# Windowed attention and a routed feed-forward: row maxima one unit further ahead, router logits in quarters, fewer signals from TensorE, a rearranged start

## The reference

```python
x = layernorm(x + attention(x))
x = layernorm(x + ffn(x))
# attention: 16 heads of 8 features, windows of 64 tokens with stride 32
# (7 windows and one more at the end, the same tokens as the seventh)
scores = einsum('bhnqd,bhnkd->bhnqk', qw, kw) * scale + pos_bias
ow = einsum('bhnqk,bhnkd->bhnqd', softmax(scores), vw)   # overlapping windows are averaged
attention = merged @ Wo + bo
# ffn: every token goes to its two best of 8 experts
logits = xt @ router_w.T
topk_vals, topk_idx = top_k(logits, 2)
g = sigmoid(topk_vals); g = g / (g.sum() + 1e-10)
h = silu(xt @ w_gate[e]) * (xt @ w_up[e])                # 256 hidden features
out += ge * (h @ w_down[e])
```

## Time and profile before

| | us |
|---|---|
| median of 3 runs | 895.55 (891.91 to 898.95) |
| profiled execution | 893.16 |
| its span, first to last instruction | 891.4 |
| TensorE busy in the span | 712.7 |
| VectorE, ScalarE, GpSimd busy | 510.3, 365.9, 429.9 |

### The profile page before, as it was taken

The page is one execution under the profiler, slowest core; times in us unless marked ns, Lnnn a source line. Parts: engine busy times, 40 slices in busy tenths (PEclk is TensorE's granted clock), DMA queues, the critical chain, the costliest instruction groups (busy, mean ns, idle before and its releaser), DMA issues. The chain is left out here.

```text
span 891.4 us, 33669 instructions
## 1 busy us (share of the span) xinstructions
PE 712.7 (80%) x13562; PEld 574.6 (64%) x13562; DVE 510.3 (57%) x1623; ACT 365.9 (41%) x546; POOL 429.9 (48%) x483
## 2 busy tenths in 40 slices
PE   5599999999899898899899998777678787787600
PEld 2376766776676776766676776677667677777500
DVE  7545665665665666666666674355543444454357
ACT  3144334334334334334334332444434455455338
POOL 8422155355355354354355443655555655555545
PEclk8899999999999999999999998788998999999955
DMA  6873443443543443544543401232223322222177
GB/s 164 246 221 93 117 124 118 125 123 116 126 124 113 129 124 113 129 125 110 132 124 114 117 22 31 74 106 60 66 77 100 95 73 73 72 74 81 42 294 280
DMA packets 84025, 103.56 MB, mean 116 GB/s; under 512 B 15936, under 2 KB 70592, under 8 KB 83872
## 3 DMA queue, kind: packets, MB, share of 16 engines
q1 hardware_dynamic: 75232, 83.57, 32.5%
q0 software_dynamic: 8640, 17.84, 6.3%
HBM read 60.12 MB, written 40.79 MB: 113 GB/s over the span
## 5 line engine op out<-in xcount | busy, mean ns | idle before, releaser
L760 DVE TENSOR_REDUCE neg_max<-score_ps 128x16 f32<-128x1024 f32 x109 | 133.4, 1223 | 142.6 <-PE score_ps L1166 139.9
L281 POOL DMA_INDIRECT slots<-rows_sb,slot_at x128 | 127.1, 993 | 159.3 <-PE o_ps L1219 133.0
L537 POOL DMA_INDIRECT results<-scaled_sb,result_at x142 | 136.2, 959 | 114.5 <-DVE scaled_sb L1029 78.5
L672 ACT ACTIVATE prob<-scoret_ps 128x1024 f32<-128x1024 f32 x112 | 114.6, 1023 | 180.6 <-PE scoret_ps L1166 177.3
L1219 PE MATMUL o_ps<-v_sb,prob 128*32 128x18 f32 x7168 | 93.2, 187 | 13.4 <-issue 13.1
L1219 PEld LDWEIGHTS o_ps<-v_sb,prob 128*32 128x32 f32 x7168 | 78.3, 110 | 26.9 <-issue 19.2
L1203 PE MATMUL scoret_ps<-max_rows,half 128*64 128x512 bf16 x448 | 69.5, 388 | 26.3 <-DMA max_rows<-maxt_sb 26.3
L705 ACT CAST w_slot<-wgu_sb 128x1024 fp32r x71 | 74.9, 1055 | 0.4 <-issue 0.3
L1166 PE MATMUL scoret_ps<-blocks,stack 128*64 128x256 f16 x920 | 71.6, 277 | 0.0
L1186 PE MATMUL scoret_ps<-bias_hl,fold 128*64 128x512 f16 x448 | 70.1, 393 | 1.7 <-issue 1.0
L1166 PE MATMUL score_ps<-blocks,stack 128*64 128x256 f16 x872 | 67.0, 274 | 2.7 <-DMA blocks<-scratch 2.7
(11 more groups left out here) (177 smaller groups left out, 1565.4 us busy)
## 6 DMA issues: line engine op xcount, KB each, us to landing
scratch<-qk_hl SPq DMA_DIRECT2D x128, 128.0 KB
stack<-scratch SPq DMA_DIRECT2D x32, 512.0 KB
blocks<-scratch SPq DMA_DIRECT2D x128, 128.0 KB
xin<-slots SPq DMA_DIRECT2D x71, 130.0 KB
blocks<-results SPq DMA_DIRECT2D x16, 512.0 KB, 6.3
x_sb<-in_x SPq DMA_DIRECT2D x16, 256.0 KB
out<-y_sb SPq DMA_DIRECT2D x16, 256.0 KB, 3.9
results<-scaled_sb,result_at POOLq DMA_INDIRECT x142
```

The lines of the kernel that those rows point to most:

```text
L281: nc.gpsimd.indirect_dma_start(slots, bass.IndirectOffsetOnAxis(ap=slot_at[:, k % 2, n:n + 1], axis=0), rows_sb[:, k % 2, n // TT, n % TT, ...
L537: pool.indirect_dma_start(results, bass.IndirectOffsetOnAxis(ap=result_at[s % RBUF][:, t:t + 1], axis=0), scaled_sb[:, s % RBUF, t, :], No ...
L672: act.activation(prob[:, (par + u) % 2, :], scoret_ps[:, :, :].rearrange("p b c -> p (b c)"), ACT.Exp).then_inc(exp_done, 1)
L760: dve.tensor_reduce(neg_max[:, par, v, :], ps[:, :, :].rearrange("p b (h k) -> p (b h) k", k=W), AX_X, ALU.max, negate=True).then_inc(max_ ...
```

## The change

- Maxima: from step 1 on, turn u has `bias_s` and `scores` of unit u + 1 instead of u, and `turn_maxima` and `max_copy` come a turn earlier. Unit 0 of the step after next is computed at the end of the last turn, on TensorE after `bias_s` and ahead of the next step's `scores_t`, on VectorE behind `places`. Step 0 keeps its order, with this last part added.
- Logits: each 128-token matmul becomes four of 32 tokens, for 32 rows of the output each.
- Feed-forward: TensorE signals twice a chunk instead of four times. `silu` waits for the end of the whole `gate_up`; `high` waits, from chunk 3 on, for `down` of three chunks earlier.
- Last step: `make_fill` first, `powers` ahead of the scatters 4 to 7.
- Start: queries and keys no longer wait for their biases; the first K split is VectorE's; half of the stores of `qk_hl` of steps 0 and 1, and two of the four first `blocks`, are issued by ScalarE; the second memset of `blocks` comes after the bias; `max_rows` is cleared by GpSimd; the wait for `constants` moves into step 0.

```diff
+        def store_half(eng, k, par, n):
+            eng.wait_ge(halves, 4 * k + 2 * n + 2)
+            eng.nop(nofuse=True)
+            for c in range(C):
+                part = c % 2 if n == 0 else c // 2
+                eng.dma_start(scratch[par, n, :, c, :, :].rearrange("j r t -> r j t"),
+                              qk_hl[:, n, part, :]).then_inc(scratched, 16)
...
 (SyncE, start)
-                halves_out(0, 0)
+                store_half(sp, 0, 0, 0)
                 landed(0)
-                stacks_s(0, 0)
+                stacks(0, 0, 0, s_stacked, range(2))
                 stacks_t(0, 0)
                 load(2, 0)
-                halves_out(1, 1)
+                store_half(sp, 1, 1, 0)
...
 (GpSimd, step)
+                    if last:
+                        make_fill()
...
-                    if last:
-                        scatter(i - 2, 4)
-                        scatter(i - 2, 5)
-                        make_fill()
                     if not first:
                         powers(i - 1)
                     if last:
-                        scatter(i - 2, 6)
-                        scatter(i - 2, 7)
+                        for n in range(TT, TOP * TT):
+                            scatter(i - 2, n)
...
 (GpSimd, start)
-                split(0)
+                split(0, (0,))
...
                 split(1)
+                pool.memset(max_rows[:, :, :], 0.0).then_inc(rows_cleared, 1)
...
 (ScalarE)
                 def high(s):
-                    act.wait_ge(xt2_ps, s + 1)
+                    if s < 3:
+                        act.wait_ge(xt2_ps, s + 1)
+                    else:
+                        act.wait_ge(y_ps, s - 2)
...
                 def silu(s):
-                    act.wait_ge(gate_ps, s + 1)
+                    act.wait_ge(up_ps, s + 1)
...
-                for k in range(2):
-                    xt_copy(k, k)
-                    qk_copy(k)
+                xt_copy(0, 0)
+                act.wait_ge(bqk_in, 32)
+                act.mul(b_qs[:, :], b_q[:, :], SCALE).then_inc(bqs_ready, 1)
+                act.wait_ge(bqs_ready, 1)
+                qk_copy(0)
+                store_half(act, 0, 0, 1)
+                xt_copy(1, 1)
+                act.wait_ge(cleared, 1)
+                act.wait_ge(scratched, 16 * 2 * C)
+                act.nop(nofuse=True)
+                for j in range(2, 4):
+                    block_in(act, 0, 0, j, s_stacked)
+                qk_copy(1)
...
+                store_half(act, 1, 1, 1)
                 all_steps(act, step)
...
 (VectorE, start)
+                clear(0)
+                dve.wait_ge(qk_copied, 2)
+                dve.wait_ge(halves, 2)
+                settle(dve)
+                dve.tensor_copy(qk_hl[:, 1, 0, :], qk_f[:, 1, :]).then_inc(halves, 1)
+                dve.wait_ge(halves, 3)
+                dve.tensor_tensor(qk_hl[:, 1, 1, :], qk_f[:, 1, :], qk_hl[:, 1, 0, :], ALU.subtract).then_inc(halves, 1)
                 dve.wait_ge(bias_in, 64)
...
-                dve.memset(max_rows[:, :, :], 0.0).then_inc(rows_cleared, 1)
+                clear(1)
...
 (VectorE, step)
                         if there(i + 1):
-                            if u < NU:
-                                maximum(i + 1, 1 - par, u)
-                            if u == NU:
+                            v = u if first else u + 1
+                            if v < NU:
+                                maximum(i + 1, 1 - par, v)
+                            if u == (NU if first else NU - 1):
                                 max_copy(i + 1)
...
                             places(i - 1, 1 - par)
+                        if u == NU + 1 and there(i + 2):
+                            maximum(i + 2, par, 0)
...
 (TensorE)
                 def logits(k):
                     pe.wait_ge(x1t_ready, k + 1)
                     for t in range(TT):
-                        last = pe.matmul(bank[1 if there(k + 1) else 0][:, t * E:(t + 1) * E], x1t_sb[:, t * P:(t + 1) * P], rw_sb[:, :],
-                                         start=True, stop=True)
+                        for quarter in range(4):
+                            rows = slice(32 * quarter, 32 * quarter + 32)
+                            last = pe.matmul(bank[1 if there(k + 1) else 0][rows, t * E:(t + 1) * E],
+                                             x1t_sb[:, t * P + 32 * quarter:t * P + 32 * quarter + 32], rw_sb[:, :],
+                                             start=True, stop=True)
...
                             scores_t(i, par, u)
-                            if there(i + 1):
-                                if u or first:
-                                    bias_s(i + 1, u)
-                                scores(i + 1, 1 - par, u)
+                            v = u if first else u + 1
+                            if there(i + 1) and v < NU:
+                                bias_s(i + 1, v)
+                                scores(i + 1, 1 - par, v)
+                        if u == (NU if first else NU - 1) and there(i + 1):
+                            turn_maxima(i + 1, 1 - par)
...
                         if u == NU and there(i + 1):
-                            turn_maxima(i + 1, 1 - par)
                             project_v(i + 1, 1 - par, 1)
...
                                 bias_s(i + 2, 0)
+                                scores(i + 2, par, 0)
...
-                    last.then_inc(xt2_ps, 1)
+                    if s < 3:
+                        last.then_inc(xt2_ps, 1)
...
-                    for n, signal in ((0, gate_ps), (1, up_ps)):
+                    for n in range(2):
...
-                        last.then_inc(signal, 1)
+                    last.then_inc(up_ps, 1)
```

More of the change, by code:

```diff
@@ L207, in build @@
         rank_ps, scattered = sem("rank_ps"), [sem(f"scattered{n}") for n in range(2)]
-        qk_in, consts_in = sem("qk_in"), sem("consts_in")
+        qk_in, bqk_in, consts_in = sem("qk_in"), sem("bqk_in"), sem("consts_in")
         ident_made, v_cleared = sem("ident_made"), sem("v_cleared")
@@ L250, in build @@
         y_out = [sem(f"y_out{n}") for n in range(4)]
-        N_QK, N_CONST = 4, 4
+        N_QK, N_CONST = 2, 4
         LINKS = 15
@@ L270, in all_steps, with block_in @@
                 step(i, i % 2, i == 0, i == STEPS - 1)
+        def store_half(eng, k, par, n):
[5 more added lines that the diff above has]
+                              qk_hl[:, n, part, :]).then_inc(scratched, 16)
+        def block_in(eng, par, n, j, signal):
+            eng.dma_start(blocks[32 * j:32 * j + 32, par, 1 - n, :, j, :],
+                          scratch[par, 1 - n, j].rearrange("c (d g) t -> (c d) g t", g=G)).then_inc(signal, 16)
         def routed(k):
@@ L307, in _ @@
                     sp.dma_start(dst[:, :], src.rearrange("(j r a) -> r j a", j=4, a=1),
-                                 allow_slow_non_contiguous=True).then_inc(qk_in, 16)
+                                 allow_slow_non_contiguous=True).then_inc(bqk_in, 16)
                 for dst, src in ((w_v, wv), (w_o, wo)):
@@ L324, in halves_out @@
                     for n in range(2):
[L325 to L330, removed]
+                        store_half(sp, k, par, n)
                 def landed(k):
@@ L334, in landed, with stacks @@
                     settle(sp)
-                def stacks(k, par, n, signal):
+                def stacks(k, par, n, signal, js=range(4)):
                     after(sp, signal, 80 * k)
@@ L344, in stacks @@
                                  scratch[par, n].rearrange("j c (d g) t -> (j c d) g t", g=G)).then_inc(signal, 16)
-                    for j in range(4):
-                        sp.dma_start(blocks[32 * j:32 * j + 32, par, 1 - n, :, j, :],
-                                     scratch[par, 1 - n, j].rearrange("c (d g) t -> (c d) g t", g=G)).then_inc(signal, 16)
+                    for j in js:
+                        block_in(sp, par, n, j, signal)
                 def stacks_s(k, par):
@@ L483, in add_bias, with split @@
                                        b_o[:, :].unsqueeze(1).to_broadcast([P, TT, P]), ALU.add).then_inc(xb_ready, 1)
-                def split(k):
+                def split(k, ns=range(2)):
                     after(pool, scratched, 16 * 2 * C * k)
-                    for n in range(2):
+                    for n in ns:
                         pool.wait_ge(qk_copied, 2 * k + n + 1)
@@ L745, in _, with clear @@
             def _(dve):
-                for par in range(2):
+                def clear(par):
                     dve.memset(blocks[:, par, :, :, :, :].rearrange("p n g j t -> p (n g j t)").bitcast(F32),
                                0.0).then_inc(cleared, 1)
+                clear(0)
[5 more added lines that the diff above has]
+                dve.tensor_tensor(qk_hl[:, 1, 1, :], qk_f[:, 1, :], qk_hl[:, 1, 0, :], ALU.subtract).then_inc(halves, 1)
                 dve.wait_ge(bias_in, 64)
@@ L1097, in project_qk @@
```

(6 more changed lines are left out.)

6 lines of the change are left out of this document (1 added, 5 removed).

## The result

The changed kernel takes 901.52 us (median of 20 runs, 892.20 to 907.82), the kernel before beside it 895.5 (20 runs, 889.99 to 903.32): ratio 1.0049, 95% interval 1.0026 to 1.0071. It is slower, by about half a per cent; the forecast was 857, with a range of 832 to 878. The profiled execution took 900.97 us, its span is 899.2.

The account below looks back on a forecast made before the run. It took TensorE's nearly gapless stream and its waits to bound attention, late signals the feed-forward. Terms -19.6, -9.8, -3.3, -0.7 and -5 sum to -38.4 from 893.16: 854.8, plus 2.4 for the median: 857 us, range 832 to 878.

Parts of the forecast that it names:

- Step boundary, -19.6: Attention step boundaries: maxima one unit ahead remove TensorE's waits, 1.4 us at each of 14 boundaries, -19.6 us.
- The work is the same, moved: Step boundary: one unit's bias and scores, 0.87 us, only change place, and a 0.49 us wait goes away.
- Logits, -9.8: Logits of each step: quartered matmuls take 0.34 us instead of 0.99, -0.65 us in 15 steps, -9.8 us.
- Start, -3.3: Start of the kernel: first row product at 37.5 us instead of 40.81, -3.3 us, bounds -1.5 and -5.
- Last step, -0.7: Last step: `powers` ahead of two scatters and a memset ends VectorE's wait in `gates`, -0.7 us, bounds 0 and -4.
- Feed-forward, -5: Feed-forward chunks: stalls shortened, 9 us gained, against 4 us for the later `high`; -5 us, bounds +15 and -40.
- fewer signals stand in the line: Feed-forward stalls: up signal is second, not third, so `hidden` starts about 0.7 us earlier; 0.4 us on average, 23 stalls.
- rival (4): Feed-forward: `silu`'s later signal lies on the path in every chunk, 0.72 us x 71 = 51 us, total 913; chance 0.04.
- (1): Feed-forward: signals are the whole story, halving them gives chunks of 3.4 us, -30 us instead of -5, total 832; chance 0.17.
- (3): Logits in quarters gain nothing, or the feed-forward loses 10 us: total 867 to 872; chance 0.12.
- (2): Boundaries: maximum behind `places`, or row transfer in the scatters' traffic, takes 1 us more; 13 us less gained, 870; chance 0.16.
- (5): Feed-forward: `silu`'s later signal costs 0.35 to 0.6 us a chunk, so the time ends within 1%; chance 0.05.

Follow-up runs that it names:

- whole 790.20: Changed kernel with the four feed-forward signals of before and the logits in 8 whole matmuls: 790.20 us, ratio 0.9748 to the kernel before.
- quarters 796.10: Changed kernel with four feed-forward signals, quartered logits and 64 empty instructions ahead of TensorE's first matmul, which left no record: 796.10 us, ratio 0.9838.
- e1: Kernel before with only the feed-forward's signals cut to two a chunk: 812.92 us, ratio 1.0035.
- the halves: Changed kernel with four feed-forward signals and the logits in 16 matmuls of 64 columns: 795.17 us, ratio 0.9829 to the kernel before.
- the best version: Changed kernel with four feed-forward signals, whole logits and the maximum of unit 0 ahead of `places`: 784.99 us, ratio 0.9694 to the kernel before.

## Why the prediction was wrong, by its steps

**Step boundary, -19.6.** The mechanism was right and so was its size as a sum of waits: they fell by 23.5 us in the two lists above, the new wait is 0.67 where 0.6 was forecast, and end of values to `project_out` is 268.78 to 273.17, 4.39 against the 4.2 worked out. What failed is the sentence "The work is the same, moved". Alone on an undisturbed chip it gave 14.4 us, with pauses of 14.0 us, against 5.4 in the trace of before on another such chip.

**Logits, -9.8.** The stretch itself is right: 0.40 us measured, 0.34 forecast. "All on TensorE's stream" was the failed step: it prices a matmul by its time in the array and not by its place in the instruction stream. Alone the quarters gave 4.2 us; beside the maxima they lost 6 (whole 790.20, quarters 796.10 on one chip), of which the traces explain no more than a part. The lower bound "nothing gained" was too high.

So the failed step of the forecast for the steps is one that it does not have, a term for TensorE's instructions: it put the pauses at nothing without a reason. On the first chip, of the 23.5 us of waits removed and about 9 us in the logits, 18.6 came back as pauses. Of this, the pauses at the ends of blocks are shown (1.2 us before, 14.8 after, from the first step to the last, by the same count). On that chip there is a second kind: mostly 0.46 to 0.5 us at a fixed place of the step some 310 matmuls behind its first row product, before and after, and in some of the changed kernel's steps once more near the 720th, as the pause of 0.47 in the boundary above. Other chips show it at most as 0.3 us now and then. The cause of this kind is open. Nor does the account close: -23.5 for the waits, -8.9 for the logits (0.59 by 15), +18.6 for the pauses and +2.5 in two waits that are new in the list (for `o_sb` and `ctxt_sb`, 1.3 and 1.2) make -11.3, and -3.9 was measured. Where these 7 us go stays open. One difference on that chip is in the semaphore events of the traces: the signal of a unit's transposed scores comes over 0.2 us late 25 times in 104 after, 9 in 105 before and not at all in the trace of before on another chip. Whether that costs anything was not tested.

**Start, -3.3.** Measured -2.3 on the first chip (38.50 for 37.5) and -2.0 (41.12 us to 39.16 in traces of two other chips). The term was slightly too large. VectorE's first maximum begins at 25.96, not at 24.4: it stands behind the second memset of `blocks`, which now comes last.
```profile
19.15 6.88 DVE L767 MEMSET blocks<- 128x8192 f32 x1 [1.77 <-issue]
25.96 1.16 DVE L786 TENSOR_REDUCE neg_max<-score_ps 128x16 f32<-128x1024 f32 x1
```
The gain comes from the shorter way from there to the row product, 12.5 us instead of 14.9. The clearing of `max_rows` that moved to GpSimd takes 6.07 us there; it took 3.04 on VectorE. Nobody waited for it.

**Last step, -0.7.** From the order of the whole it can't be told apart; the start and the last step together gave 5.3 us alone, where 4.0 was forecast.

**Feed-forward, -5.** Wrong in sign, and inside the bounds: +11 us for the chunks on the first chip. There the stalls stay as they were the earlier trace rows. The prediction's reading of them, a signal of TensorE that arrives late, is borne out by the semaphore events of the trace: the gate's matmul was over at 739.34, the next event of its semaphore is at 743.75, and `silu` starts at 743.77. `silu` after:
```profile
745.50 0.60 ACT L725 ACTIVATE silu_sb<-scoret_ps 128x512 f32<-128x512 f32 x1 [4.38 <-remote]
```
The failed step here is "fewer signals stand in the line". With half the signals as many come late: the up half's is over 0.5 us late in 39 of 69 chunks, and in 42 of 68 before. TensorE is busy for 213.5 us in the chunks instead of 206.9, at the granted clock of 0.87 instead of 0.92, which is 6.6 of the 11 us; whether the clock fell because of the waits or for another reason is not shown. On the other chips these stalls don't exist: the gate's and up half's signals are 0.014 us behind their matmul, before has no wait of TensorE for `h_sb` in its rows there, and its chunks take 187.8 us, not 267.6:
```profile
L1309 PE MATMUL bank<-ident,xin x142: 270/272/476, 555.9 to 743.7; 128*128 128x128 f32 x142
```
Even so the two signals cost 3.0 to 4.6 us: e1's chunks take 192.8. The Trainium skill's price of a semaphore increment ("TensorE: Matmul & The Clock Gate", "The cost: per-tile semaphore tail") would have made them a gain of 3.7 us; no run shows one. In size that is rival (4) at 0.05 us a chunk, far under its 0.72. That the cost comes from waiting for a later signal than before fits it, and is argued.

**The rivals.** (1) is refuted. Of (3) the second part came true, the chunks lost 11 us; the first, quarters that gain nothing, did beside the maxima and not alone. In (2) the second wait did not grow. (5), within 1%, is where the time ended, but by another mechanism. That the profile before showed pauses of TensorE (10.6 us in 42 to 530) was in the list I read. I left them out since the change did not name them, and the queue "instruction" was on the page.

## What to carry to other kernels

Where TensorE is busy nearly without a gap, look at its instructions, not only its time: splitting a matmul into short ones, or removing waits around short ones, can hand part of the gain to the instruction stream. Look for idle time put down to "issue" inside a group of equal matmuls, and count the records up to it. Test parts in company too: two changes that gained 14.4 and 4.2 us alone gave 4 to 6 together. And leave out a signal only where what waits for it had to wait for the later event anyway.

## What the runs showed of the hardware

- The instruction stream makes pauses of 0.3 to 2.8 us at ends of blocks of 256 records of TensorE: at some 3 of 88 block ends in the steps of before, at some 20 of 90 in those of the changed kernel. At none of 1907 block ends did TensorE go on sooner than 1.0 us after the end of the block's packet. The Trainium skill ("Runtime: NRT & Kernel Launch", "Instruction fetch mechanics") has the block of 256 instructions, and the trace agrees (16.4 KB a packet, pauses whole multiples of 256 records apart, to within one). It also says that the fetch is hidden by the rate at which instructions are issued. The traces here disagree, with up to 22.5 us of pauses at block ends in 488 (the halves).
- Chips differ by a tenth on the same kernel: 895.5 us on one and 807.1 to 811.8 on four others. Of the 82 us between the two traces of before, 80 lie in the chunks (267.6 and 187.8 us). On the slow one `silu` idles over 4 us at a time while GpSimd issues indirect transfers, though the matmul it waits for is long over the earlier trace rows; on the others it does not. The semaphore events show TensorE's signals late there: the gate's by more than 0.5 us in 44 of 69 chunks of before (up to 7.0 us), and in none in three traces from other chips. What delays them was not tested, since no experiment ran on that chip. Whether the best version gains there is open as well.
